# A transformer block on eight Trainium2 cores: the coupling network's last layer and the layer norm's scaling are issued at other places

## The reference, cut to what matters

```python
xn = _layernorm(x)                                   # x: (8, 2048, 1024)
q, k, v = proj(Wq), proj(Wk), proj(Wv)               # 16 heads of 64
w = jax.nn.sigmoid(q @ k.T * SCALE); w = w / (w.sum(-1) + EPS)
attn = (w @ v) @ Wo.T
gf = _global_net(xn.mean(axis=1))                    # one number per sequence
out = xn
for _ in range(3):                                   # NUM_CYCLES
    h = gelu(out @ w1 + b1)                          # 1024 -> 1024
    h = gelu(h @ w2 + b2)                            # 1024 -> 512
    h = gelu(h @ w3 + b3)                            # 512 -> 256
    tf = sigmoid(h @ w4 + b4)                        # 256 -> 1
    coupling = 0.1 + adaptive_range * (0.7*gf + 0.3*tf - 0.5) * 2.0
    out = out + coupling * _twist(out)
return x + attn + out
```

## Time and profile before

| | us |
|---|---|
| timed runs, median of 2 | 3999.87 (3854.89 and 4144.85) |
| the profiled execution, its own time | 3704.89 |
| its span, slowest core (core 7) | 3703.3 |
| spans of the eight cores | 3696.5 to 3703.3 |
| mean granted TensorE clock of the cores | 0.953 to 0.955 |

### The profile page before, as it was taken

How to read it: one execution, slowest core, us unless ns; L and a number is a source line. 1 busy time by engine, 2 the same in 40 slices (tenths; PEclk the granted TensorE clock), 3 DMA queues, 4 the chain that set the end, 5 groups by cost and what they waited for, 6 DMA issues and landing times.

```text
span 3703.3 us, 42764 instructions; the slowest of 8 cores (3696.5 to 3703.3 us)
## 1 busy us (share of the span) xinstructions
PE 3316.7 (90%) x14180; PEld 1762.0 (48%) x14180; DVE 938.9 (25%) x1563; ACT 1044.1 (28%) x1907; POOL 36.0 (1%) x16
## 2 busy tenths in 40 slices
PE   1489989999999999899999999968999999999995
PEld 0143333333333333333333333427777777777772
DVE  4412222222222222222222120031222222222224
ACT  3414424324234244243242341001222222222220
POOL 0000000000000000000000000021000000000000
PEclk9999999999999999999999999989999999999995
DMA  4000000000000000000000000001000000000006
GB/s 120 1 29 18 1 17 1 1 18 1 1 18 1 1 18 1 18 1 1 18 1 1 1 1 12 17 29 52 1 1 1 1 1 1 1 1 1 1 1 182
DMA packets 88587, 54.19 MB, mean 15 GB/s; under 512 B 2242, under 2 KB 86338, under 8 KB 88386
## 3 DMA queue, kind: packets, MB, share of 16 engines
q1 hardware_dynamic: 71746, 43.07, 4.0%
q10 hardware_dynamic: 16640, 8.39, 0.8%
HBM read 43.07 MB, written 8.39 MB: 14 GB/s over the span
## 4 chain that ended last, share of the span: by engine, by line
PE 87%; ACT 4%; DVE 3%; issue 3%; DMA 2%; ACTq 0%; DVEq 0%; SPq 0%
PE p L66 87%; DMA slotB<-x 2%; ACT slotC L66 2%; DVE slotC L66 2%; DVE slotA L66 1%; ACT L66 1%; DVE slotB L66 1%; ACT slotA L66 0%; ACT wblk L66 0%; ACT tf_sb L66 0%; DVE cp_sb L66 0%; DVEq L56 0%; ACTq L56 0%; DMA wblk<-w 0%; DMA wblk<-wvT 0%
## 5 line engine op out<-in xcount | busy, mean ns | idle before, releaser
L66 PE MATMUL p<-slotC 128*128 128x512 f16 (+1 forms) x4096 | 1346.1, 489 | 17.0 <-DVE slotC L66 16.0
L66 PE MATMUL p<-slotA 128*128 128x256 f16 (+1 forms) x6144 | 896.3, 310 | 39.1 <-DVE slotA L66 38.2
L66 PEld LDWEIGHTS p<-slotC 128*128 128x128 f16 (+1 forms) x4096 | 479.6, 118 | 874.4 <-issue 678.5
L66 PEld LDWEIGHTS p<-slotA 128*128 128x128 f16 (+1 forms) x6144 | 777.0, 127 | 160.2 <-issue 51.8
L66 ACT ACTIVATE slotC<-p 128x512 f32<-128x512 f32 x1024 | 611.4, 597 | 786.3 <-PE p L66 786.3
L66 PE MATMUL p<-slotA,slotC 128*128 128x512 f16 x2304 | 517.4, 387 | 38.6 <-DVE slotC L66 38.5
L66 PEld LDWEIGHTS p<-slotA,slotC 128*128 128x128 f16 x2304 | 227.2, 99 | 327.2 <-issue 69.8
L66 PE MATMUL p<-identb,slotC 128*128 128x128 f32 x384 | 134.3, 394 | 190.3 <-ACT slotC L66 102.7
L66 DVE RECIPROCAL slotC<-p 64x512 f32<-64x512 f32 x64 | 214.4, 3350 | 317.0 <-PE p L66 316.2
L66 PE MATMUL p<-slotB,wblk 128*128 128x512 f32 x512 | 221.4, 595 | 4.5 <-DVE slotB L66 4.5
L66 DVE TENSOR_SCALAR slotC<-p 1x512 f32<-1x512 f32 x64 | 43.8, 685 | 678.5 <-PE p L66 678.5
(11 more groups left out here) (57 smaller groups left out, 922.8 us busy)
## 6 DMA issues: line engine op xcount, KB each, us to landing
slotB<-x SPq DMA_DIRECT2D x1, 8192.0 KB, 31.5
slotB<-x ACTq DMA_DIRECT2D x16, 512.0 KB, 5.5
out<-slotB SPq DMA_DIRECT2D x16, 512.0 KB, 3.8
wblk<-wqT SPq DMA_DIRECT2D x8, 512.0 KB, 5.1
wblk<-wkT SPq DMA_DIRECT2D x8, 512.0 KB, 4.1
wblk<-wvT SPq DMA_DIRECT2D x8, 512.0 KB, 4.1
wblk<-woT SPq DMA_DIRECT2D x8, 512.0 KB, 3.9
wblk<-w SPq DMA_DIRECT2D x8, 512.0 KB, 4.1
```

Of the source, the lines that this page charges most:

```text
L66: return Inst(getattr(real, op)(*a, **k) if real is not None else None)
```

## The change

Two things move, and nothing is added or taken away.

In the layer norm, the scaling of tiles 0 and 1 is issued ahead of the loop, and the scaling of tile t+2 at the end of tile t's turn (behind its casts and ahead of those of tile t+1).

In the coupling network, `emit_cn1` can now issue a part of the chunks. Chunk 0 of the next tile's w1 layer is issued first, then the w4 layer of this tile with its sigmoid and scaling, and then chunks 1 to 7.

```diff
-            for t in range(NTT):
+            def emit_xnt(t):
                 xt = B[:, t * 1024:(t + 1) * 1024]
-                xnt = ln_xnt[t % 2]
                 Sc.wait(sV, ln_done)
                 Sc.waits(xnt_free[t % 2])
-                Sc.activation(xnt[:, :], xt, AF.Identity,
...
+                state[("xnt_ready", t)] = sS.n
+
+            emit_xnt(0)
+            emit_xnt(1)
+            for t in range(NTT):
+                xnt = ln_xnt[t % 2]
+                xnt_ready = state[("xnt_ready", t)]
                 for c in range(NCH):
...
                 xnt_free[t % 2] = [(sT, sT.n)]
+                if t + 2 < NTT:
+                    emit_xnt(t + 2)
...
-            def emit_cn1(cy, ti):
-                for oc in range(NCH):
+            def emit_cn1(cy, ti, ocs=range(NCH)):
+                for oc in ocs:
...
-                state["g1_ready"] = sS.n
-                state["cn1_done"] = sT.n
+                if list(ocs)[-1] == NCH - 1:
+                    state["g1_ready"] = sS.n
+                    state["cn1_done"] = sT.n
...
                     if nxt is not None:
                         emit_s16(*nxt)
-                        emit_cn1(*nxt)
+                        emit_cn1(*nxt, ocs=range(0, 1))
 
                     b7 = bacq(7)
...
                     cp_ready = sV.n
+                    if nxt is not None:
+                        emit_cn1(*nxt, ocs=range(1, NCH))
```

More of the change, by code:

```diff
@@ L178, in emit @@
             bank_free = {i: [] for i in range(8)}
+            state = {}
             def bacq(i):
@@ L255, in split16 @@
                 return sV.n
-            state = {"g": 0, "pending": None, "qrep_free": [[], []],
-                     "qrep_done": [0, 0], "qrep_next": None, "carry": None,
-                     "tail": None, "sig_free": [[], [], []]}
+            state.update({"g": 0, "pending": None, "qrep_free": [[], []],
+                          "qrep_done": [0, 0], "qrep_next": None, "carry": None,
+                          "tail": None, "sig_free": [[], [], []]})
             def load_split_pair(pair, guard_mark):
@@ L272, in emit @@
             xn_marks = []
-            for t in range(NTT):
+            def emit_xnt(t):
                 xt = B[:, t * 1024:(t + 1) * 1024]
-                xnt = ln_xnt[t % 2]
                 Sc.wait(sV, ln_done)
                 Sc.waits(xnt_free[t % 2])
-                Sc.activation(xnt[:, :], xt, AF.Identity,
-                              bias=ln_nmr[:, t:t + 1], scale=ln_rstd[:, t:t + 1]).inc(sS)
-                xnt_ready = sS.n
+                Sc.activation(ln_xnt[t % 2][:, :], xt, AF.Identity,
+                              bias=ln_nmr[:, t:t + 1],
+                              scale=ln_rstd[:, t:t + 1]).inc(sS)
+                state[("xnt_ready", t)] = sS.n
[4 more added lines that the diff above has]
+                xnt_ready = state[("xnt_ready", t)]
                 for c in range(NCH):
```

## The result

| | before | after |
|---|---|---|
| median of all runs, us | 3856.34 (10 runs) | 3675.18 (11 runs) |
| lowest | 3703.26 | 3581.72 |
| ratio of the runs that can be compared | | 0.9672, 95% interval 0.9657 to 0.9688 |
| profiled execution: time, span | 3704.89, 3703.3 | 3583.84, 3582.3 |
| mean granted clock, core by core | 0.953 to 0.955 | 0.969 to 0.970 |

The change is 3.3% faster. Some cores had stretches of lower clock in six of the ten runs of before, in six of the eleven after and in nearly all of the experiments', so the ratio leaves such runs out, and what follows compares cores without them, called undisturbed.

What follows compares the result with a forecast made beforehand. The prediction took TensorE as the bound, with 24 pauses that also lower its clock. From a 3703.3 us span it took 112.9 (coupling network) and 12.8 (layer norm), added 1.6 outside the span: 3579 us, range 3555 to 3880.

Steps and rivals of the forecast that it cites:

- What bounds the kernel: Whole kernel: TensorE, busy 90% of the span, so only shortening its work or its pauses pays.
- the 24 pauses: Coupling network: TensorE stood 64.5 us waiting for the coupling numbers; each costs idleness and a half-speed start of w2.
- The coupling network: Period between w4 layers falls from 46.16 to 41.25 us, 4.91 less, 23 times: 112.9 us.
- the eighth Gelu's wait: Between w1's end and w2's start: 0.88 us as in the first iteration, with the broadcast inside; bounds 0.88 to 1.6.
- What is queued behind the moved work: ScalarE's reloaded Gelu and VectorE's split for the next tile stay hidden in the coupling network, at no cost.
- The room of 0.5 us for the reloaded Gelu: Coupling network: chunk 1's Gelu ends at 4.7 us after w4, its bank is wanted by chunk 3 at 5.28.
- The layer norm: At 15 tile ends the next transposes come sooner, 0.90 less 0.05 us each: 12.8 us; bounds 0 and 13.5.
- The sum: Whole kernel: span 3577.6 us plus 1.6 outside it, 3579 us against 3704.9, 3.4% faster.
- Reload: Coupling network rival: table switches stall w1 by 1.0 us per iteration, 23 in all, giving 3602 us; 7 in 100.
- The clock falls all the same: Coupling network rival: w2 stays at 17.11 us, only 2.63 per iteration goes, giving 3632 us; 12 in 100.
- The layer norm gains nothing: Layer norm rival: ScalarE is in the way of its own casts, giving 3592 us; 5 in 100.
- The other side: Coupling stage rival: without rests the chip grants less clock; at 0.80, 3811 us, 2.9% slower; 5 in 100.

Runs made afterwards that it cites:

- x4: Changed kernel plus an unused 128-value sigmoid that w2 and the broadcast wait for, restoring the old pause: 3712.8 us, estimated 3684 without its disturbed stretch.
- x2: Only the layer norm's part of the change, the coupling network issued as before: undisturbed cores 3683.5 to 3690.2 us.
- x1: Only the coupling network's part of the change, the layer norm issued as before: undisturbed cores 3586.6 to 3595.0 us.
- x8: Changed kernel with w4 ahead of the last two w1 chunks: periods 41.41 or 41.42 us but one; core 0 took 3663.8 us with three disturbed stretches.
- x3: Changed kernel with w4 ahead of the last w1 chunk in place of chunk 1: undisturbed cores 3640.5 to 3649.2 us.
- x7: Changed kernel plus per-Gelu waits in w2 and w3, layer-norm transposes through eight banks, attention's row-sum matmul in bank 7: undisturbed cores 3427.1 to 3432.8 us.

## What the prediction had right, and the step that failed

*What bounds the kernel.* Right. The two readings on which all hung were the 24 pauses and the clock behind them, and x4 shows that the pause brings the clock down.

*The coupling network.* The term was 23 x 4.91 = 112.9 us; measured are 23 x (46.16 - 41.44) = 108.6. The pieces: w2 with its wait 14.83 predicted, 2987.17 - 2972.35 = 14.82 measured; the eighth Gelu's wait came as in the first iteration, 0.26 us of idleness behind the broadcast; the difference is the w4 layer. I took 0.90, from w3's spacing, with bounds 0.88 to 1.10. It costs 1.05, within the bounds: its four records hold the queue for 3450.23 - 3449.27 = 0.96, and the w1 layer, cut in two, takes 2.71 + 18.44 = 21.15, 0.09 more than the 21.06 between its start and w4's before. 23 x 0.15 = 3.5 us of the 4.3 missing are this.

*What is queued behind the moved work.* Right. VectorE's split ends 2980.89 + 2.29 - 2971.39 = 11.8 us behind the broadcast's start and is wanted after 2990.70 - 2971.39 = 19.3, against 11.8 and 19.2 predicted. The room of 0.5 us for the reloaded Gelu held: its bank was wanted some 0.5 us behind its end, and no wait shows. The activation starts 1.29 to 1.30 us after its load's start here too (2998.70 - 2997.41). The drain that the Trainium skill adds to the load ("ScalarE: Activation LUTs", What ACT_TABLE_LOAD costs) does not show in this kernel.

*The layer norm.* 12.8 us predicted. From the first pair behind the start-up wait to the next stage, before and now:

```profile
66.50 0.87 PE L66 MATMUL p<-identb,slotC 128*128 128x128 f32 x2 [6.84 <-DVE slotA L66]
...
192.36 3.54 PE L66 MATMUL p<-gcin,wblk 128*128 128x1 f32 x16 [1.80 <-DVE gcin L66]
```

```profile
66.07 0.88 PE L66 MATMUL p<-identb,slotC 128*128 128x128 f32 x2 [7.07 <-DVE slotA L66]
...
179.44 3.54 PE L66 MATMUL p<-gcin,wblk 128*128 128x1 f32 x16 [1.76 <-DVE gcin L66]
```

That is 125.86 us and now 113.37, 12.5 less. In x2 the same stretch is 113.35, in x1 125.94. The stage behind attention starts 2504.53 - 2491.74 = 12.79 us earlier, but that such a number equals 12.8 is luck, since the cores of one execution start that stage up to 7 us apart.

*The sum.* 3579 us predicted, 3583.84 for the profiled execution, a ratio of 0.966 (3579 / 3704.9) against 0.9672 measured. Of the 4.7 us that the span is over the sum, 4.3 are the coupling network's and 0.3 the layer norm's.

*Where it failed: the step from the profiled execution to the time that is told.* The sum starts from 3704.9, a profiled execution with no disturbed core, and 3579 was then put down as the time, with nothing added for disturbed runs. The time it stands against, 3999.87, was such a lifted one, the median of two disturbed runs. So the lift was a term that I knew of and put at nothing on one side only. I wrote that if the changed kernel's runs were lifted as the two known ones, by 4 to 12%, they would lie at 3720 to 4005, gave that "not quite half a chance", and used it only for the range. The runs show a lift on both sides, and a smaller one. The median of before fell to 3856.34 with eight more runs, 4.1% above its profiled execution. That of the changed kernel is 3675.18, 2.5% above its own, the least lifted of its six disturbed runs out of eleven. Set beside 3999.87 my number says 10.5% faster, where the kernel is 3.3% faster. The ratio was the quantity that the profile could give, and the absolute time wasn't. That 3675.18 lies inside the range is the work of the room left for the lift, and not of the sum.

*The rivals.* Reload: did not happen (x8, and the row above). The clock falls all the same: did not happen at 0.96 us, but x3 shows how near it was, since with 2.21 us from the broadcast to w2, 1.2 more, it is back in most iterations. The layer norm gains nothing: false. The other side, a chip that grants less because the rests are gone: in the profiled execution the clock is 1.00 over the 996 us, and the undisturbed runs are as short. Whether more runs are disturbed after the change can't be told from six of ten and six of eleven.

## What to carry to other kernels

Read the granted clock right behind every repeated pause of TensorE: here pauses of 2.5 to 2.7 us cost nearly as much again in the half-speed matmuls that follow, pauses of 5.5 us a third more, and both go together when one independent piece of work is kept back to be issued into the detour over the other engines. Put the detour where two or more chunks stand behind it and not one, since the table reload that follows it makes the next Gelu late. And forecast a ratio from a profile: an absolute time needs, in addition, a term for how the runs differ from the profiled one.

## What the runs showed of the hardware that I had not expected

The disturbed cores have a sharp signature. In x8, core 0, two stretches of attention that do the same kind of work (windows, columns as in the earlier trace rows):

```profile
541.00:700.00 159.00, 159.00 (x397) 51.71 (x396) 35.23 (x42) 57.31 (x96) 0.00 (x0) 0.81 0.00 1
815.00:1000.00 185.00, 185.00 (x589) 66.85 (x588) 45.31 (x52) 76.88 (x130) 0.00 (x0) 1.00 0.02 6
```

The clock is 0.81 for about 160 us and then whole again. Core 0 of x8 had three such stretches and took 3663.8 us; its code apart from w4's place is that of the changed kernel, whose core 0 took 3577.1, so each cost (3663.8 - 3577.1) / 3 = 29 us. Core 7 of x7 gives 28: 3489.2 us with two, 3432.4 without any. These are estimates, since cores differ by some us from run to run. By their spans, pairs of cores (0 and 1, 2 and 3, and so on) had them together. In the slowest run of x7 cores 0 to 3 had a mean clock of 0.81 over the whole span (4071.6 to 4076.0 us), so the level can also last. The Trainium skill ("TensorE: Matmul & The Clock Gate", Seeing it yourself) describes a level of 13/16, 0.81, for dies with three or more cores in dense matmuls. The level agrees, but here it mostly came in bouts of some 160 us, on some pairs of cores and not on others, and in some runs on none. What starts a bout stays open. So does why, in x3, the same pause cost nothing in six iterations of core 0 and 1.7 us in each later one.
